# Mixer stage: value and gate projections placed between halves of the small inverse products, first batch's head products moved ahead, decay products moved from VectorE to GpSimd

## The chip, the cores and the metric

The kernel runs on one core of one Trainium2 chip. The metric is the device time of one execution in microseconds. TensorE is called PE here, VectorE DVE, ScalarE ACT, GpSimd POOL and SyncE, which issues most loads, SP.

## The reference, cut to what matters

The program is a two-layer model on two sequences (B = 2) of 128 positions and width 512, in fp32. Layer 0 has a cross-attention, a *mixer* (a gated delta rule with 16 heads of width 32) and a mixture of experts. Layer 1 has two more attentions and a feed-forward. The change is in the mixer alone. What it computes, per head:

```python
q, k, v = silu(conv(xn @ Wq)), silu(conv(xn @ Wk)), silu(conv(xn @ Wv))   # causal conv, 4 taps
q, k    = rope(l2norm(q)), rope(l2norm(k))
decay   = exp(cumulated -softplus(xn @ Wgk + dt_bias) * exp(A_log))
beta    = sigmoid(xn @ Wb + bb)
# S_t = decay_t * S_(t-1);  S_t += beta_t * k_t (v_t - S_t^T k_t)^T;  o_t = S_t^T q_t
out     = (rmsnorm(o) * gnorm_w * silu(xn @ Wg)) @ Wo
```

The kernel doesn't run the recurrence over t. For each head it forms the 128x128 matrix of key products times decay, solves a triangular system for the updates in four blocks of 32 positions (with the inverses of the 32x32 diagonal blocks computed ahead), and then multiplies by the query products times decay.

## The kernel before, in words

Each engine has its own instruction stream, written out by hand in the order in which it runs: `mixer_pe`, `mixer_act`, `mixer_dve`, `mixer_pool`. Semaphores order the engines among each other. Nothing is reordered by a scheduler, so an engine that waits holds back all that is behind it in its stream.

**Projections.** `project_mix(pe, m, cc, c)` (line 1016) is one matmul 128x128 by 128x256. m is 0 for keys, 1 for queries, 2 for values, 3 for the gate; cc is the chunk of 128 output channels (four of them), c the input chunk (four). An fp32 matmul appears in the trace as two matmul and two weight-load records, so one m is 16 matmuls and 32 records, under line 1022. The results go to PSUM banks named by `MIX_BANK`: m = 2 and m = 3 both use banks 6 and 7 before. ACT evacuates m = 1 and 2 (lines 1231, 1232), DVE runs the convolution's other taps on them (line 1303), ACT applies SiLU (line 1237). Gate chunks go through SiLU on ACT straight out of PSUM (line 1277).

**Small inverse products.** There are 128 diagonal blocks of 32x32 (`M` = 32 per group of 32 partitions). DVE inverts their 16x16 halves by columns (lines 1364, 1365), then two PE passes join the halves: `cross_rows` (line 1062) and, after a copy (line 1370), `cross_inverse` (line 1072), each 128 matmuls of 16 columns, 256 records. DVE subtracts the result (line 1374). Before, `cross_rows` stands ahead of the values' projection, and `cross_inverse` in its middle.

**Decay.** `dec` is built by PE (lines 1135, 1136) into banks 0 to 3 in turn and by ACT's Exp (line 1269). The same banks are used later.

**Head products.** `head_products(right, b)` (line 1052) multiplies krot by krot (kk) or by qrot (qk) for batch b: 16 matmuls, 32 records, into four banks (4b to 4b+3 before). DVE multiplies kk by decay (`um_dve`, line 1322), ACT copies qk out of PSUM (line 1283, four copies per batch), and DVE multiplies that by decay (`pm_dve`, line 1328, four instructions 128x1024). Before, kk of both batches and then qk of both batches stand behind the gate's projection.

**The blocked solve.** Four levels a = 0 to 3, each for both batches: `earlier` (PE, line 1167), `rest_dve` (line 1345), `within` (PE, line 1179), `solved_dve` (line 1353). Level 0 has `within` and `solved` alone. One level is 2 x 32 records of `earlier` and 2 x 32 of `within`. `pm_dve` stands in DVE's stream between `rest` and `solved` of each level, the fourth one behind the last level. The outputs (line 1200, 64 records) need pm and the last level's solution; norm, gate and the output projection (lines 1205 to 1222) follow, then the mixture of experts.

**Loads.** SP loads blocks of weights of 1 MB into a ring of four buffers (line 222); a block is requested when `blk_used` says that the one in its place has been used.

## Time and profile before

| | us |
|---|---|
| three runs | 1354.48, 1353.78, 1358.29 |
| median | 1354.48 |
| span of the profiled execution | 1357.6 |
| mixer, first instruction on PE to last of line 1222 | about 559 to 670 |
| PE busy over the span | 1313.1 (97%) |
| DVE busy | 926.7 (68%) |
| ACT busy | 718.1 (53%) |
| POOL busy | 19.2 (1%) |

The page doesn't say which of the three runs is the profiled one; its span of 1357.6 us lies 0.7 us below the longest of them. Times of trace rows are in microseconds from the span's start. In a row of a timeline the first number is the start, the second the time covered, "x" the number of records, and the bracket the idle time of the engine ahead of it with what ended it ("issue" is idle time in which no semaphore and no data was waited for). PE busy includes records that run at the lower granted clock.

### The profile page before, as it was taken

How to read it: one execution, taken by the hardware profiler on the slowest of the kernel's cores; microseconds unless marked ns; L12 is line 12 of the kernel's file. 1: busy time of each engine (PE TensorE's matmuls, PEld its weight loads, DVE VectorE, ACT ScalarE, POOL GpSimd, SP SyncE). 2: the span in 40 equal slices, each digit the busy share in tenths (PEclk: the TensorE clock that was granted, in tenths of full speed). 3: DMA queues.
4: the chain of work that ended last, by engine and by line, in shares of the span. 5: the costliest groups of instructions: out<-in, count | busy, mean ns of one | idle time of the engine just before them, and what ended most of it. 6: DMA issues, size and time to landing. Idle time of an engine off the chain costs nothing.

```text
span 1357.6 us, 23877 instructions
## 1 busy us (share of the span) xinstructions
PE 1313.1 (97%) x9930; PEld 1112.1 (82%) x9930; DVE 926.7 (68%) x1209; ACT 718.1 (53%) x887; POOL 19.2 (1%) x20
## 2 busy tenths in 40 slices
PE   9999999999999999887999999999988999999998
PEld 8899999989999996766677888888765789888886
DVE  4666665676665666675779999999777677555553
ACT  5544444554444443372357777777654444665552
POOL 0000000000000000000000000000011010000000
PEclk9999999999999999898799999999998999999999
DMA  8111011311010011201058999999960145555552
GB/s 293 38 31 36 20 36 45 124 39 36 21 36 21 21 63 63 93 34 64 33 196 332 358 351 347 346 352 344 367 259 16 63 155 187 186 185 186 185 185 78
DMA packets 50223, 197.72 MB, mean 146 GB/s; under 512 B 12112, under 2 KB 20560, under 8 KB 30416
## 3 DMA queue, kind: packets, MB, share of 16 engines
q1 hardware_dynamic: 47792, 187.41, 38.1%
q0 software_dynamic: 2336, 8.91, 1.8%
q8 instruction: 75, 1.23, 0.4%
q14 instruction: 20, 0.16, 0.0%
HBM read 195.78 MB, written 0.52 MB: 145 GB/s over the span
## 4 chain that ended last, share of the span: by engine, by line
PE 86%; DVE 8%; ACT 3%; issue 2%; DMA 1%; SPq 0%; POOL 0%; DVEq 0%; ACTq 0%
PE psum L465 13%; PE psum L435 13%; PE psum L2445 9%; PE psum L1641 8%; PE psum L492 5%; PE psum L2446 4%; PE psum L1664 4%; PE psum L517 4%; PE psum L1644 4%; PE psum L2428 3%; PE psum L1022 2%; PE psum L1667 2%; PE psum L2459 2%; PE psum L476 1%; PE psum L1678 1%
## 5 line engine op out<-in xcount | busy, mean ns | idle before, releaser
L1710 DVE TENSOR_TENSOR arena_r<-ring,arena_r 128x2048 fp32r<-128x2048 f32 x96 | 219.7, 2290 | 29.6 <-ACT arena_r L1704 29.3
L465 PE MATMUL psum<-ring_r,arena_r 128*128 128x256 f32 x1536 | 198.1, 287 | 0.7 <-DVE ring_r L300 0.7
L1704 ACT CAST arena_r<-ring 128x2048 fp32r<-128x2048 f32 x96 | 183.4, 1914 | 14.1 <-PE psum L1644 11.1
L465 PEld LDWEIGHTS psum<-ring_r,arena_r 128*128 128x128 f32 x1536 | 188.6, 191 | 1.3 <-DVE ring_r L300 1.1
L435 PE MATMUL psum<-arena_r 128*128 128x512 f32 x768 | 183.5, 394 | 0.4 <-ACT arena_r L751 0.3
L2445 PE MATMUL psum<-arena_r 128*128 128x512 f32 x512 | 181.0, 399 | 1.4 <-DVE arena_r L2510 1.4
L435 PEld LDWEIGHTS psum<-arena_r 128*128 128x128 f32 x768 | 141.6, 188 | 32.0 <-DVE arena_r L300 1.0
L2446 PE MATMUL psum<-arena_r 128*128 128x256 f32 x512 | 143.9, 281 | 0.0
L2399 DVE TENSOR_TENSOR arena_r<-ring,arena_r 128x2048 fp32r<-128x2048 f32 x43 | 98.6, 2293 | 62.1 <-ACT arena_r L2394 62.1
L1641 PE MATMUL psum<-arena_r 128*128 128x512 f32 x512 | 129.5, 395 | 1.3 <-issue 1.3
L2445 PEld LDWEIGHTS psum<-arena_r 128*128 128x128 f32 x512 | 96.3, 188 | 25.3 <-DVE arena_r L2510 1.5
L1641 PEld LDWEIGHTS psum<-arena_r 128*128 128x128 f32 x512 | 94.2, 188 | 20.4 <-issue 1.7
L772 ACT COPY arena<-psum 128x1024 f32<-128x1024 f32 x64 | 61.7, 1016 | 89.6 <-PE psum L492 89.6
L300 DVE TENSOR_TENSOR arena_r<-arena,arena_r 128x2048 fp32r<-128x2048 f32 (+4 forms) x34 | 52.1, 1538 | 79.2 <-ACT arena_r L743 52.2
L2394 ACT CAST arena_r<-ring 128x2048 fp32r<-128x2048 f32 x44 | 84.0, 1909 | 30.3 <-PE psum L2428 20.0
L2446 PEld LDWEIGHTS psum<-arena_r 128*128 128x128 f32 x512 | 96.8, 189 | 0.0
L637 DVE TENSOR_TENSOR arena<-arena,psum 128x1024 f32<-128x1024 f32 x64 | 75.2, 1216 | 24.8 <-PE psum L506 24.8
L764 ACT COPY ring<-psum 128x512 f32<-128x512 f32 x64 | 37.2, 582 | 78.7 <-PE psum L465 78.7
L779 ACT ACTIVATE arena<-arena 128x1024 f32<-128x1024 f32 x64 | 66.3, 1058 | 21.0 <-DVE arena L637 19.7
L617 DVE TENSOR_TENSOR arena<-arena 128x512 f32<-128x512 f32 (+1 forms) x128 | 71.5, 559 | 4.4
L1644 PE MATMUL psum<-arena_r 128*128 128x512 f32 x256 | 68.6, 390 | 0.0
L492 PEld LDWEIGHTS psum<-arena 64*128 64x128 f32 x1024 | 59.7, 188 | 9.9 <-issue 9.1
(337 smaller groups left out, 1900.3 us busy)
## 6 DMA issues: line engine op xcount, KB each, us to landing
ring<-in_stream SPq DMA_DIRECT2D x151, 1024.0 KB, 4.9
arena<-in_ctxT POOLq DMA_DIRECT2D x8, 1024.0 KB, 11.6
arena<-in_ctxT SPq DMA_DIRECT2D x7, 1024.0 KB, 7.9
arena<-in_wk SPq DMA_DIRECT2D x16, 256.0 KB, 3.2
wv_in<-in_wv SPq DMA_DIRECT2D x8, 512.0 KB, 3.5
arena<-in_wq SPq DMA_DIRECT2D x16, 256.0 KB, 2.7
arena<-in_wk SPq DMA_DIRECT2D x16, 128.0 KB, 3.2
arena<-in_wo SPq DMA_DIRECT2D x2, 1024.0 KB, 6.5
```

Of the source, the lines that this page charges most:

```text
L435: last = nc.tensor.matmul(bank, wk_sb[wp][:, c, w], cx[xp][kb][:, c, :], start=c == wp == xp == 0, stop=c == C - 1 and xp == 1)
L465: last = nc.tensor.matmul(bank[:, q * T:(q + 1) * T], cx[xp][kc // 4][:, c, kc % 4 * P:(kc % 4 + 1) * P], wv_sb[wp][:, c, :], start=c == w ...
L492: last = nc.tensor.matmul(psum[:, 2 * half + kc // 4, kc % 4 * P:kc % 4 * P + P], kT[j % 2][a:a + 64, k0:k0 + P], qT[a:a + 64, j % 2, half ...
L637: nc.vector.tensor_tensor(part, part, per_row(psum[:, SPREAD_BANK, 0:P], KC // 2), ALU.subtract).then_inc(shifted, 1)
L1641: nc.tensor.matmul(out, xg[xp][:, c, e, :], hi[:, c, :], start=c == xp == 0, stop=False)
L1644: last = nc.tensor.matmul(out, xg[0][:, c, e, :], lo[:, c, :], start=False, stop=c == C - 1)
L1704: nc.scalar.copy(mwhi[p % MB], ring[k % RING][:, :]).then_inc(moe_hi, 1)
L1710: nc.vector.tensor_tensor(mwlo[p % MB], ring[(BLK_MOE + p) % RING][:, :], mwhi[p % MB].bitcast(fp32), ALU.subtract).then_inc(moe_lo if p < ...
L2394: nc.scalar.copy(whi[j % 2], ring[k % RING][:, :]).then_inc(w_hi, 1)
L2399: nc.vector.tensor_tensor(wlo[j % 2], ring[(BLK_W12 + j) % RING][:, :], whi[j % 2].bitcast(fp32), ALU.subtract).then_inc(w_lo, 1)
L2445: nc.tensor.matmul(psum[:, 4 + s, :], w[0][:, c, :], src[:, :, c, :], start=c == 0, stop=False)
L2446: last = nc.tensor.matmul(psum[:, 4 + s, 0:T], w[1][:, c, :], src[:, 0, c, :], start=False, stop=c == FC - 1)
```

## The change

In words:

- PE's stream: the first chunk of the values' projection goes ahead of `cross_rows`; `cross_rows` and `cross_inverse` are cut in halves of 64 matmuls (128 records), with one chunk of a projection between the halves; turning of the queries (`turn_mix`) goes behind the whole values' projection; kk and qk of batch 0 go ahead of and behind the gate's last chunk, kk of batch 1 follows, qk of batch 1 is last.
- PSUM: the gate goes to banks 2 and 3, the inverse products to banks 0 and 1, and the batches swap places (`BASE` = (4, 0)).
- ACT's stream: the copy between the two inverse products moves from DVE to ACT; the query squares go between the evacuations; the first half of the gate's SiLU goes ahead of the values' SiLU.
- DVE's stream: the rotation of the queries goes between the halves of the values' convolution; `um_dve` of batch 0 goes ahead of the inverse's last subtraction and of `vp_dve`; `pm_dve` is gone.
- POOL's stream: `pm_pool`, the same four multiplications, behind the memsets.

```diff
-        MIX_BANK = (4, 6, 6, 6)
+        MIX_BANK = (4, 6, 6, 2)
+        ROWS_BANK, INV_BANK = 0, 1
+        BASE = (4, 0)
...
             nc.gpsimd.memset(cross_sb[:, :, HK:], 0.0).then_inc(xf_clear, 1)
+            for n in range(4):
+                pm_pool(gp, n)
...
+            if m == 2 and c == 0 and cc % 2 == 0:
+                pe.wait_ge(mix_evac, C + cc + 2)
+            if m == 3 and cc == c == 0:
+                pe.wait_ge(dec_exp, G)
...
-                    last = nc.tensor.matmul(psum[:, 4 * b + i, cc * P:(cc + 1) * P], krot[r, cc, b, :], right[r, cc, b, :],
+                    last = nc.tensor.matmul(psum[:, BASE[b] + i, cc * P:(cc + 1) * P], krot[r, cc, b, :], right[r, cc, b, :],
...
+            def project_whole(m, cc):
+                for c in range(C):
+                    project_mix(pe, m, cc, c)
+
+            halves = (range(0, M // 2), range(M // 2, M))
+            project_whole(2, 0)
             pe.wait_ge(xt_ready, 1)
-            cross_rows(4).then_inc(inv_filled, 1)
-            pe.wait_ge(mix_evac, 2 * C)
-            for cc in range(C):
-                if cc == C // 2:
-                    pe.wait_ge(xt_ready, 2)
-                    cross_inverse(5).then_inc(inv_filled, 1)
-                for c in range(C):
-                    project_mix(pe, 2, cc, c)
+            pe.wait_ge(dec_exp, 5)
+            cross_rows(ROWS_BANK, halves[0])
+            project_whole(2, 1)
+            cross_rows(ROWS_BANK, halves[1]).then_inc(inv_filled, 1)
+            project_whole(2, 2)
+            project_whole(2, 3)
+            turn_mix(pe, 1, 4)
+            pe.wait_ge(xt_ready, 2)
+            pe.wait_ge(dec_exp, 6)
+            cross_inverse(INV_BANK, halves[0])
+            project_whole(3, 0)
+            cross_inverse(INV_BANK, halves[1]).then_inc(inv_filled, 1)
+            project_whole(3, 1)
+            project_whole(3, 2)
+            pe.wait_ge(mix_evac, 3 * C)
+            pe.wait_ge(rope_ready, 2)
+            head_products(krot, 0).then_inc(kk_filled, 1)
+            project_whole(3, 3)
+            pe.wait_ge(um_ready, 1)
+            head_products(qrot, 0).then_inc(qk_filled, 1)
+            pe.wait_ge(mix_gs, 2)
             pe.wait_ge(xt_ready, 3)
-            turn_mix(pe, 1, 4)
-            pe.wait_ge(mix_evac, 3 * C)
-            for cc in range(C):
-                for c in range(C):
-                    project_mix(pe, 3, cc, c)
-            pe.wait_ge(dec_exp, G)
-            head_products(krot, 0).then_inc(kk_filled, 1)
-            pe.wait_ge(mix_gs, 2)
-            pe.wait_ge(rope_ready, 2)
             head_products(krot, 1).then_inc(kk_filled, 1)
-            for b in range(B):
-                pe.wait_ge(um_ready, b + 1)
-                head_products(qrot, b).then_inc(qk_filled, 1)
+            pe.wait_ge(um_ready, 2)
+            head_products(qrot, 1).then_inc(qk_filled, 1)
...
             silu_mix_act(act, 1)
+            act.wait_ge(inv_filled, 1)
+            act.wait_ge(xf_clear, 3)
+            nc.scalar.copy(cross_sb[:, :, 0:HK], psum[:, ROWS_BANK, :].rearrange("p (n j) -> p n j", j=HK)).then_inc(xt_ready, 1)
+            evac_mix_act(act, 2, 0)
+            evac_mix_act(act, 2, 1)
             square_mix_act(act, 1, 1)
-            for cc in range(C):
-                evac_mix_act(act, 2, cc)
+            evac_mix_act(act, 2, 2)
+            evac_mix_act(act, 2, 3)
+
+            def gate_act(i):
+                wait_mix_chunk(act, 3, 2 * i + 1)
+                nc.scalar.activation(gsT[:, 2 * i:2 * i + 2, :, :], psum[:, MIX_BANK[3] + i, :].rearrange("p (c b t) -> p c b t", c=2, b=B),
+                                     ACT.Silu).then_inc(mix_gs, 1)
+
+            gate_act(0)
             silu_mix_act(act, 2)
...
+            gate_act(1)
...
-        def pm_dve(dve, n):
+        def pm_pool(gp, n):
 
             heads = slice(n * H // 2, (n + 1) * H // 2)
-            dve.wait_ge(qk_copied, 4 * (n // 2) + 4)
-            nc.vector.tensor_tensor(pm[:, heads, :], qk[:, heads, :], dec[:, heads, :], ALU.mult).then_inc(pm_ready, 1)
+            gp.wait_ge(qk_copied, 4 * (n // 2) + 4)
+            nc.gpsimd.tensor_tensor(pm[:, heads, :], qk[:, heads, :], dec[:, heads, :], ALU.mult).then_inc(pm_ready, 1)
...
             conv_mix_dve(dve, 1, 1)
-            cross_copy_dve(dve)
             rope_start_dve(dve, 1, qrot)
+            conv_mix_dve(dve, 2, 0)
+            rope_dve(dve, 1, qrot, 4)
+            conv_mix_dve(dve, 2, 1)
+            um_dve(dve, 0)
             cross_inverse_dve(dve)
-            conv_mix_dve(dve, 2, 0)
-            conv_mix_dve(dve, 2, 1)
-            rope_dve(dve, 1, qrot, 4)
             vp_dve(dve)
-            um_dve(dve, 0)
             um_dve(dve, 1)
             for a in range(NT):
                 for b in range(B):
                     if a:
                         rest_dve(dve, a, b)
-                if a:
-                    pm_dve(dve, a - 1)
                 for b in range(B):
                     solved_dve(dve, a, b)
-            pm_dve(dve, 3)
```

Every other `4 * b` in a PSUM bank's number of the mixer becomes `BASE[b]`.

## Rows read from the trace of the kernel before

**Rows 1.** The page: span, and queue of instruction loads (packets, MB, share)

```profile
span 1357.6 us, 23877 instructions
...
q8 instruction: 75, 1.23, 0.4%
```

**Rows 2.** Timeline of PE, 598 to 640 us: start, time covered, instructions, idle before

```profile
600.33 2.22 PE L1062 MATMUL psum<-arena 16*32 16x16 f32 x139 [0.81 <-DVE arena L1420]
603.93 1.91 PE L1062 MATMUL psum<-arena 16*32 16x16 f32 x117 [1.38 <-issue]
605.76 6.28 PE L1022 MATMUL psum<-xnT,ring 128*128 128x256 f32 x16
611.97 2.29 PE L1072 MATMUL psum<-arena 32*32 32x16 f32 x251
616.57 0.24 PE L1072 MATMUL psum<-arena 32*32 32x16 f32 x5 [2.31 <-issue]
616.75 5.41 PE L1022 MATMUL psum<-xnT,ring 128*128 128x256 f32 x16
621.99 1.88 PE L1031 MATMUL psum<-arena,cst 128*128 128x512 f32 x4
623.71 7.09 PE L1022 MATMUL psum<-xnT,ring 128*128 128x256 f32 x32
630.73 2.07 PE L1052 MATMUL psum<-arena 32*128 32x128 f32 x64
...
635.51 1.17 PE L1052 MATMUL psum<-arena 32*128 32x128 f32 x32 [0.49 <-DVE arena L1322]
```

**Rows 3.** Windows: us, PE, PEld, DVE, ACT, POOL busy, granted clock, DMA share, GB/s

```profile
601.00:601.50 0.50, 0.50 (x50) 0.50 (x44) 0.50 (x3) 0.45 (x1) 0.00 (x0) 1.00 0.14 33
...
643.60:644.10 0.50, 0.50 (x32) 0.47 (x32) 0.50 (x1) 0.00 (x0) 0.00 (x0) 0.50 0.17 33
647.40:647.90 0.50, 0.50 (x42) 0.42 (x36) 0.33 (x2) 0.00 (x0) 0.00 (x0) 0.50 0.17 33
...
574.00:600.00 26.00, 23.53 (x402) 16.38 (x401) 19.90 (x47) 23.37 (x55) 0.00 (x0) 1.00 0.19 70
...
604.20:610.80 6.60, 6.60 (x124) 5.58 (x117) 2.62 (x5) 2.11 (x2) 0.00 (x0) 0.50 0.02 5
```

**Rows 4.** Timeline of DVE and ACT, 598 to 662 us

```profile
629.73 1.22 DVE L1341 TENSOR_TENSOR arena<-arena,nkp 128x1024 f32<-128x1024 f32 x1
632.04 3.42 DVE L1322 TENSOR_TENSOR arena<-psum,arena 96x1536 f32<-96x1536 f32 x2 [1.09 <-PE psum L1052]
...
635.09 4.01 ACT L1283 COPY arena<-psum 128x512 f32<-128x512 f32 x8 [3.65 <-PE psum L1052]
...
645.08 1.22 DVE L1328 TENSOR_TENSOR arena<-arena 128x1024 f32<-128x1024 f32 x1
646.33 1.29 DVE L1353 TENSOR_TENSOR arena<-psum,beta 32x512 f32<-32x512 f32 x2
```

**Rows 5.** Timeline of PE, 639 to 662 us

```profile
643.55 1.25 PE L1167 MATMUL psum<-arena 64*32 64x32 f32 x64 [1.17 <-DVE arena L1353]
...
647.08 1.26 PE L1167 MATMUL psum<-arena 96*32 96x32 f32 x64 [1.17 <-DVE arena L1353]
...
650.70 3.73 PE L1200 MATMUL psum<-arena 128*32 128x128 f32 x64 [1.27 <-DVE arena L1353]
```

**Rows 6.** Timeline of POOL and DVE around the only other SBUF-to-SBUF products on POOL

```profile
674.88 2.71 POOL L2624 TENSOR_TENSOR arena_r<-xn,arena_r 128x1024 fp32r<-128x1024 f32 x1 [115.26 <-ACT arena_r L1718]
...
1086.69 0.61 DVE L2339 SCALAR_TENSOR_TENSOR arena<-arena,lkvs 128x128 f32<-128x128 f32 x2
1087.15 4.53 POOL L2638 TENSOR_TENSOR arena_r<-ring,arena_r 128x2048 fp32r<-128x2048 f32 x1 [56.40 <-ACT arena_r L2394]
...
1087.89 4.20 DVE L2339 SCALAR_TENSOR_TENSOR arena<-arena,lkvs 128x128 f32<-128x128 f32 x2
```

**Rows 7.** Windows of the mixture of experts, columns as in rows 3

```profile
740.00:780.00 40.00, 40.00 (x185) 32.47 (x184) 35.53 (x24) 31.06 (x25) 0.00 (x0) 1.00 0.94 352
```

More of the change, by code:

```diff
@@ L1051, in head_products, with cross_rows @@
                     r = tile_rows(i)
-                    last = nc.tensor.matmul(psum[:, 4 * b + i, cc * P:(cc + 1) * P], krot[r, cc, b, :], right[r, cc, b, :],
+                    last = nc.tensor.matmul(psum[:, BASE[b] + i, cc * P:(cc + 1) * P], krot[r, cc, b, :], right[r, cc, b, :],
                                             start=True, stop=True)
             return last
-        def cross_rows(bank):
-            for n in range(M):
+        def cross_rows(bank, tiles):
+            for n in tiles:
                 for i in range(4):
@@ L1064, in cross_rows, with cross_inverse @@
             return last
-        def cross_inverse(bank):
-            for n in range(M):
+        def cross_inverse(bank, tiles):
+            for n in tiles:
                 for i in range(4):
@@ L1166, in earlier @@
                         h = 4 * cc + i
-                        last = nc.tensor.matmul(psum[tile_rows(i), 4 * b, cc * DK:(cc + 1) * DK], um[0:DK * a, b * H + h, tile_rows(a)],
+                        last = nc.tensor.matmul(psum[tile_rows(i), BASE[b], cc * DK:(cc + 1) * DK], um[0:DK * a, b * H + h, tile_rows(a)],
                                                 xw[0:DK * a, b, h * DK:(h + 1) * DK], start=True, stop=True)
@@ L1178, in within @@
                         r = tile_rows(i)
-                        last = nc.tensor.matmul(psum[tile_rows(a), 4 * b + i, cc * DK:(cc + 1) * DK], xt[r, :, (cc * B + b) * NT + a],
+                        last = nc.tensor.matmul(psum[tile_rows(a), BASE[b] + i, cc * DK:(cc + 1) * DK], xt[r, :, (cc * B + b) * NT + a],
                                                 rhs[r, b, cc, :] if a else vp[r, cc, b, 0, :], start=True, stop=True)
@@ L1199, in mixer_pe @@
                         h = 4 * cc + i
-                        last = nc.tensor.matmul(psum[tile_rows(i), 4 * b, cc * P:(cc + 1) * P], xw[:, b, h * DK:(h + 1) * DK],
+                        last = nc.tensor.matmul(psum[tile_rows(i), BASE[b], cc * P:(cc + 1) * P], xw[:, b, h * DK:(h + 1) * DK],
                                                 pm[:, b * H + h, :], start=True, stop=True)
@@ L1208, in mixer_pe @@
                 for cc in range(C):
-                    last = nc.tensor.matmul(psum[0:H, 4 * b + 1, 0:P], C_("sums")[:, cc * H:(cc + 1) * H], osq[:, b, cc, :],
+                    last = nc.tensor.matmul(psum[0:H, BASE[b] + 1, 0:P], C_("sums")[:, cc * H:(cc + 1) * H], osq[:, b, cc, :],
                                             start=False, stop=cc == C - 1)
@@ L1214, in mixer_pe @@
                 for cc in range(C):
-                    last = nc.tensor.matmul(psum[:, 4 * b + 1, cc * P:(cc + 1) * P], C_(f"heads{cc}")[0:H, :], rs[0:H, b * P:(b + 1) * P],
+                    last = nc.tensor.matmul(psum[:, BASE[b] + 1, cc * P:(cc + 1) * P], C_(f"heads{cc}")[0:H, :], rs[0:H, b * P:(b + 1) * P],
                                             start=True, stop=True)
@@ L1270, in mixer_act @@
             silu_mix_act(act, 1)
-            square_mix_act(act, 1, 1)
-            for cc in range(C):
-                evac_mix_act(act, 2, cc)
+            act.wait_ge(inv_filled, 1)
[3 more added lines that the diff above has]
+            evac_mix_act(act, 2, 1)
+            square_mix_act(act, 1, 1)
+            evac_mix_act(act, 2, 2)
[5 more added lines that the diff above has]
+            gate_act(0)
             silu_mix_act(act, 2)
-            for i in range(2):
-                wait_mix_chunk(act, 3, 2 * i + 1)
-                nc.scalar.activation(gsT[:, 2 * i:2 * i + 2, :, :], psum[:, 6 + i, :].rearrange("p (c b t) -> p c b t", c=2, b=B),
-                                     ACT.Silu).then_inc(mix_gs, 1)
+            gate_act(1)
             for b in range(B):
@@ L1444, in mixer_dve @@
                     dve.wait_ge(mix_gs, 2)
[L1445 removed]
+                nc.vector.scalar_tensor_tensor(t1[:, :, b, :], bank4(BASE[b]), gcol[:, 0:1], gsT[:, :, b, :], ALU.mult, ALU.mult)
             for b in range(B):
```

23 lines of the change are left out of this document (9 added, 14 removed).

## The prediction

> **What bounds the kernel now.** The page comes first: 97% of the span is PE busy, but the change touches only the mixer, some 110 us of 1357.6 [rows 1], so the page's shares decide nothing. I then read the windows and the timeline of PE in the mixer. In the mixture of experts behind it PE is busy 40.00 of 40 us [rows 7], and its weights are loaded as buffers come free; it does not catch up on a late mixer, and a mixer that ends earlier should move it whole. So the question is when the outputs' products (line 1200) end, at 654.43 us [rows 5].
>
> From 599.52 us (the last decay matmul's end, 600.33 less 0.81 of idle [rows 2]) to there, PE's order is a single path with these losses [rows 2]:
> - 0.81 us waiting for DVE's last transpose, ahead of the first inverse products;
> - 1.38 us idle within them and 2.31 us within the second ones, both put down to "issue": no semaphore, no data. The first stops after 140 records, the second after 251;
> - the granted clock is 0.50 (1.2 GHz) from 604.2 to 610.8 us [rows 3], right behind the first idle stretch, and, by the durations, for a part of the time behind the second. Eight matmuls (16 records) of the values' projection take 6.28 us there and 5.41 us the second time, against 7.09 us for sixteen of the gate's at full clock [rows 2]: 0.785 and 0.68 against 0.443 us each.
>
> What is an "issue" stop? The page shows 75 packets of 1.23 MB in an instruction queue, 16.4 KB each [rows 1]. One lies in 601.0 to 601.5 (33 GB/s over half a microsecond, nothing else moving), and PE goes on at 603.93 [rows 2, 3]. Between the two stops are 117 + 16 + 251 = 384 records of each kind [rows 2], and three further packets: one packet is about 128 pairs of matmul and weight load. So I read it thus: PE holds two pages of 128 pairs; when it enters one, the next is ordered, and that one is there some 3.7 us after the entry (packet about 1 us after the entry, ready 2.7 us after the packet). In the solve's levels packets lie in 643.6 to 644.1 and 647.4 to 647.9, again 3.5 to 3.9 us apart [rows 3]. A page with 128 inverse products is eaten in 2.0 us (16 ns a pair, 2.22/139) or 1.1 us (2.29/251) [rows 2], and then PE stands.
>
> **The projections between the halves.** A half is 128 pairs; a projection chunk is 8 pairs and 4 x 0.443 = 1.77 us at full clock. The new path, marks in us of this trace:
> - 599.52 to 601.3: first values' chunk. It fills the 0.81 wait.
> - first half of the rows: 2.05, to 603.35. The page ends 3 pairs into the next chunk and the following is ready at about 603.9 (entered as before). Chunk to 605.1, second half's first 123 pairs to 607.1, next page at 607.6, half ends at 607.7.
> - two chunks 3.55 and the turning 1.72 (1.88 less the overlap of the first): 613.0. First half of the inverse, 1.15, to 614.1; gate's chunk to 615.9; 94 pairs of the second half to 616.7; the page entered at about 613.6 gives 617.3; done at 617.6.
> - two gate chunks to 621.1, kk of batch 0 1.15 to 622.3, last gate chunk to 624.1.
> So all four projections' chunks and one kk are behind PE at 624.1, where the kernel before ends the gate at 630.8 [rows 2]. What is left of stops is 0.5 + 0.6 us, against 3.7. The saving needs the clock to stay high, which I come to below.
>
> **Head products.** The first multiplication on DVE (half of 3.42, 1.7 us [rows 4]) runs beside the last gate chunk: 622.4 to 624.1. Then qk of batch 0 624.2 to 625.4, its ACT copies (half of 4.01) to 627.4; kk of batch 1 to 626.5. On DVE the inverse's subtraction (0.7, half the elements of a 1.22), a transpose and a scaling of 128x1024 (1.22 each, 1.25 taken for the first) [rows 4] stand ahead of the second multiplication: 627.4 to 629.1. Before, that DVE work lay hidden under the gate's projection; now its second part is on the path. qk of batch 1 then ends at 630.35 (before: 635.51 + 1.17 = 636.68 [rows 2]), its copies at 632.45 (639.1). The lead is 6.6 us: the head products' reorder itself saves 1.15 us of PE and one multiplication's wait, and pays part of it back to DVE's order.
>
> **Moved for nothing.** The copy on ACT costs 0.6 there, as a 128x512 read of PSUM by ACT does, and DVE isn't needed; ACT's evacuations behind it are late by that and DVE's convolution has about 4 us left before kk of batch 0 is there. Banks: 0 and 1 are free after the fifth and sixth Exp, long done; 2 and 3 after the eighth, done at 600.2. The loads requested when a projection is done come 6 to 10 us sooner and collide with nothing.
>
> **Decay products on POOL.** DVE does them in 1.22 each [rows 4]; POOL took 2.71 for the same shape [rows 6]. The first two start at 627.4 and end at 632.8, the others end by 638.3, and the outputs want them at 642 or later: hidden, with 4 us to spare. On DVE each of the three inside the levels is on the path. Level to level is 647.08 - 643.55 = 3.53 us [rows 5]. Without the product I make it 2.65: half each of earlier's 1.25, within's (about as long: as many records) and solved's 1.29 make 1.87 [rows 4, 5], a rest of 0.3 (a quarter-size piece, by the 1.22), and four hand-overs of 0.12 (estimates). That would give 3 x 0.88 = 2.6 us. But a level is 128 pairs, one page. Its packets are already 3.5 to 3.9 us apart, and the page for level 3, ready near 646.5, was only 0.5 us ahead of its use at 647.08. At 2.65 us a level PE eats faster than pages come. By my count page ends lie 5 pairs into levels 1, 2 and 3 and into the outputs; pages come at 629.0, 636.7, 640.4 and 644.1. Level 0 is solved at 633.9, level 1 at 636.55; level 2 waits for 636.7, ends at 639.8; level 3 waits for 640.4 and ends at 643.5; the outputs wait for 644.1 and, 59 of 64 pairs at 58 ns, end at 647.55. So I take 0.3 us for the move out of DVE, between 0 (the page period) and 2.6 (none).
>
> **The sum.** 654.43 - 647.55 = 6.9 us. Profile: span 1357.6 - 6.9 = 1350.7. The median of the runs shown lies 3.1 under the span, so 1354.48 - 6.9 = 1347.6 us.
>
> **Two rules of the Trainium skill.** The page of before has DVE's line 2339 at 4.20 us for two instructions beside a product on POOL that runs 1087.15 to 1091.68, and 0.61 us without it [rows 6]. By the Trainium skill, SBUF — State Buffer, Who interferes with whom, a DVE instruction with two SBUF inputs and a POOL instruction that reads SBUF exclude each other for the whole instruction. By that rule, the trace agrees, line 1341 is the one at risk here; it would start 1.3 us ahead of POOL's first product, so POOL would wait and nothing be lost, while the solve's DVE steps each read PSUM and have one SBUF input.
> The Trainium skill, Runtime: NRT & Kernel Launch, Instruction fetch mechanics, says PE holds 128 KiB of instructions and that crossing a 16 KiB boundary is mostly hidden. The stops [rows 2] speak against it; if it held in the new order, the result would be rival A's.
>
> **Rivals.**
> A. *Pages don't bind the new order* (the ordering starts earlier in a page than I think, or two may be under way). Then the stops of 0.5 + 0.6 go and the levels run at 2.65: the outputs end near 645 - 0.6 = 644.4, gain 10: 1344.5. For it: my count of page ends may be off by some pairs, and PE idles before level 0, so pages can be full. Against: the even distances of the packets.
> B. *The clock falls again.* The fall at 604.2 follows a stretch with products of 16 columns and idle time, and these products are still there. If the chunk behind the first half and the two behind it run at 0.785, 12 x 0.342 = 4.1 us go, or 2 to 4 when only some do: gain 3 to 5, 1350.5. Against: 574 to 600 us has small products, an idle 2 us and granted clock 1.00 throughout [rows 3].
> C. *The changed order does nothing*: solve and DVE's order take back what PE gains, since um of batch 1 now stands behind vp and inverse. If silu or the rotation is late too by 4 us, kk of batch 0 waits, gain 0 to 3: 1353. Against: rows show those DVE pieces short.
> D. *Slower.* The interleaving turns a burst of low activity into a lasting one, and the granted clock stays 0.50 through all 32 matmuls of values and gate: 32 x 0.342 = 10.9 us, less the 6.9: 4.0 us slower, 1358.5. It decides from 6.9/0.342 = 20 matmuls at the low clock on. Against: the projections alone, dense, raised the clock after 610.8 [rows 3].
>
> **Chances.** My forecast (gain 5.5 to 8.5) 0.42, A 0.18, B 0.24, C 0.11, D 0.05. Three runs of before spread over 0.33%, so 0.3%, 4.1 us, is what can be told from no change. Faster by more: forecast, A and about 0.16 of B: 0.76. Within: the rest of B and C: 0.19. Slower: 0.05. The range leaves out A's far end and D: 1343.0 to 1353.0; my forecast's own is 1346 to 1349.
>
> **What would show it.** Timeline of PE: values' first chunk at 599.5 without a wait; no issue stop over 1 us in the inverse products; gate done near 624; qk of batch 1 ended near 630.4. Windows: granted clock 1.00 from 600 to 628 (B: 0.50 somewhere in 604 to 611). In the levels, issue stops ahead of line 1167 or inside it, packets 3.7 apart and 3.5 to 3.7 us a level (A: 2.65). POOL: four products near 2.7 each; if any ends behind level 3, the decay products are on the path. It is wrong if the mixture of experts starts 7 us earlier and the total doesn't fall by as much.

## The result and the profile after

The changed kernel took 1350.37 us, median of nine runs (1346.89 to 1353.59), against 1355.87 for the kernel before, median of nine beside it (1351.94 to 1358.69): 5.5 us less, ratio 0.996 with a 95% interval of 0.9945 to 0.9975. Timed a second time it gave 1350.49 against 1356.15, ratio 0.9965 (0.9949 to 0.998). The forecast was 6.9 us less. In time it was 1347.6 us, with 1346 to 1349 as its own range: the measured 1350.37 is inside the range for the total (1343.0 to 1353.0) and above the forecast's own. Of the 2.8 us between them 1.4 is the baseline, three runs of the kernel before having a median of 1354.48 and nine one of 1355.87. One of the twelve executions of the changed kernel's second timing took 3289.45 us and is in no ratio; the median without it is 1350.22.

The profiled execution of the changed kernel has a span of 1347.7 us, 9.9 us under the one of before [rows 1]. Of these 7.2 us lie in the mixer between the start of its first matmuls (559.36 before, 560.03 now) and the end of the outputs' products. Only 5.0 of the 7.2 lie behind the last decay matmul, where the forecast's sum begins (+54.91 against +49.94 in the table below); PE's order ahead of it is the same in both kernels. The rest lies elsewhere; a second pair of profiles, below, shows that a good part of it is not the change's.

PE's timeline of the mixer in the changed kernel's first profile, in the place of [rows 2, 5] (start, time covered, instructions, idle before):

```profile
597.85 1.89 PE L1030 MATMUL psum<-xnT,ring 128*128 128x256 f32 x8
599.67 2.01 PE L1070 MATMUL psum<-arena 16*32 16x16 f32 x128
601.61 1.99 PE L1030 MATMUL psum<-xnT,ring 128*128 128x256 f32 x8
603.54 2.02 PE L1070 MATMUL psum<-arena 16*32 16x16 f32 x128
...
610.85 1.27 PE L1080 MATMUL psum<-arena 32*32 32x16 f32 x128
...
613.98 0.97 PE L1080 MATMUL psum<-arena 32*32 32x16 f32 x93
616.13 0.49 PE L1080 MATMUL psum<-arena 32*32 32x16 f32 x35 [1.18 <-issue]
616.55 5.41 PE L1030 MATMUL psum<-xnT,ring 128*128 128x256 f32 x16
...
629.74 1.24 PE L1060 MATMUL psum<-arena 32*128 32x128 f32 x32 [2.73 <-DVE arena L1350]
...
636.51 0.32 PE L1186 MATMUL psum<-arena 64*32 64x32 f32 x4 [0.16 <-DVE arena L1381]
637.03 1.07 PE L1186 MATMUL psum<-arena 64*32 64x32 f32 x60 [0.20 <-issue]
...
639.54 0.32 PE L1186 MATMUL psum<-arena 96*32 96x32 f32 x4 [0.35 <-DVE arena L1381]
640.77 1.07 PE L1186 MATMUL psum<-arena 96*32 96x32 f32 x60 [0.90 <-issue]
...
643.39 0.64 PE L1219 MATMUL psum<-arena 128*32 128x128 f32 x4 [0.45 <-DVE arena L1381]
644.33 3.41 PE L1219 MATMUL psum<-arena 128*32 128x128 f32 x58 [0.30 <-issue]
```

An "issue stop" is idle time of PE inside a run of its instructions that no semaphore and no data explains. The first inverse products run without one, their wait and the 1.38 us are gone; in the second the stop is 1.18 us instead of 2.31. In the levels there are now issue stops that [rows 5] do not have, each after exactly four records of `earlier`, and again after four of the outputs. Windows of the changed kernel (columns as in rows 3) show where the clock was low, right behind the stop in the second inverse, and a 16 KB packet (33 GB/s over half a microsecond) ahead of the last two stops:

```profile
617.00:620.40 3.40, 3.40 (x10) 2.74 (x9) 0.00 (x0) 0.50 (x2) 0.00 (x0) 0.51 0.02 5
...
638.00:638.50 0.50, 0.50 (x36) 0.45 (x34) 0.29 (x1) 0.00 (x0) 0.00 (x0) 0.50 0.17 33
641.60:642.10 0.50, 0.50 (x35) 0.41 (x29) 0.36 (x2) 0.00 (x0) 0.00 (x0) 0.50 0.15 33
```

DVE and POOL, in the place of [rows 4, 6]: the second multiplication starts behind the inverse's subtraction, transpose and scaling; two decay products take 4.65 us on POOL, 2.33 each, and the other two as long from 633.15.

```profile
623.13 1.75 DVE L1350 TENSOR_TENSOR arena<-psum,arena 96x1536 f32<-96x1536 f32 x1 [7.31 <-PE psum L1060]
624.81 0.67 DVE L1397 TENSOR_TENSOR arena<-arena,psum 128x512 f32<-128x512 f32 x1
625.40 1.23 DVE L1368 STREAM_TRANSPOSE arena<-arena 128x1024 f32<-128x1024 f32 x1
626.67 1.23 DVE L1369 TENSOR_TENSOR arena<-arena,nkp 128x1024 f32<-128x1024 f32 x1
627.93 1.75 DVE L1350 TENSOR_TENSOR arena<-psum,arena 96x1536 f32<-96x1536 f32 x1
...
628.31 4.65 POOL L1356 TENSOR_TENSOR arena<-arena 128x1024 f32<-128x1024 f32 x2 [68.02 <-ACT arena L1311]
```

### The profile page after: what moved, and what is told of

It is laid out like the page before. It is cut to its first block, busy times and chain, and to the rows that moved or that the text cites. A ratio compares the mean times of both kernels' runs of the same rounds, so it can differ in the third digit from the quotient of the medians.

```text
span 1347.7 us, 23879 instructions
## 1 busy us (share of the span) xinstructions
PE 1307.0 (97%) x9930; PEld 1107.0 (82%) x9930; DVE 921.4 (68%) x1204; ACT 718.7 (53%) x888; POOL 28.5 (2%) x24
## 3 DMA queue, kind: packets, MB, share of 16 engines
q8 instruction: 75, 1.23, 0.4%
## 4 chain that ended last, share of the span: by engine, by line
PE 87%; DVE 7%; ACT 2%; issue 2%; DMA 2%; SPq 0%; POOL 0%; DVEq 0%; ACTq 0%
PE psum L465 13%; PE psum L435 13%; PE psum L2464 9%; PE psum L1660 8%; PE psum L492 5%; PE psum L2465 5%; PE psum L1683 4%; PE psum L517 4%; PE psum L1663 4%; PE psum L2447 3%; PE psum L1030 2%; PE psum L1686 2%; PE psum L2478 2%; PE psum L476 1%; PE psum L1697 1%
## 5 line engine op out<-in xcount | busy, mean ns | idle before, releaser
L1729 DVE TENSOR_TENSOR arena_r<-ring,arena_r 128x2048 fp32r<-128x2048 f32 x96 | 219.7, 2290 | 29.6 <-ACT arena_r L1723 29.4
```

Source lines behind the costliest of these rows:

```text
L1729: nc.vector.tensor_tensor(mwlo[p % MB], ring[(BLK_MOE + p) % RING][:, :], mwhi[p % MB].bitcast(fp32), ALU.subtract).then_inc(moe_lo if p < ...
```

## The experiments

Ten kernels were run, the two known ones among them; nine were timed in several rounds, each beside runs of the kernel before on its chip, and its ratio is to those. Medians taken beside different runs of the kernel before are compared by ratio, since that kernel's own medians went from 1353.13 to 1356.15 between them. Marks of one profile each are taken from PE's timeline: D is the end of the last decay matmul; then, after D, the end of the gate's projection (G), of batch 1's qk (Q) and of the outputs' products (O). "Start to O" begins at the mixer's first matmuls. The table is made of starts plus durations.

| kernel | G | Q | O | start to O | median, us | ratio to before (95%) |
|---|---|---|---|---|---|---|
| before, 1st profile | 31.28 | 37.16 | 54.91 | 95.07 | 1355.87 | |
| before, 2nd profile | 29.10 | 34.99 | 52.69 | 92.86 | 1355.75 | 1.0002 (0.9983-1.0021) |
| changed, 1st profile | 26.97 | 32.97 | 49.94 | 87.92 | 1350.37 | 0.996 (0.9945-0.9975) |
| changed, 2nd profile | 25.00 | 31.58 | 47.84 | 87.57 | 1350.49 | 0.9965 (0.9949-0.998) |
| e1 products back on DVE | 26.96 | 32.88 | 50.36 | 88.75 | 1353.27 | 0.9991 (0.9974-1.0007) |
| e2 inverses in one piece | 29.66 | 35.58 | 52.65 | 93.04 | 1356.76 | 1.0017 (0.9998-1.0036) |
| e3 head products late | 23.70 | 29.58 | 46.82 | 85.20 | 1348.99 | 0.9956 (0.9937-0.9975) |
| e4 before, products on POOL | 27.58 | 33.46 | 50.26 | 90.03 | 1353.68 | 0.9991 (0.9975-1.0007) |
| e5 page ends shifted | 27.49 | 33.48 | 49.65 | 91.37 | 1354.1 (one run) | |
| e6 quarters | 24.37 | 31.21 | 48.81 | 86.97 | 1349.24 | 0.9966 (0.995-0.9983) |
| e8 late heads and quarters | 23.26 | 29.08 | 46.49 | 84.34 | 1345.93 | 0.9935 (0.9915-0.9955) |
| e9 e8 and tile products spread | 23.26 | 29.08 | 45.60 | 85.75 | 1345.69 | 0.9944 (0.9924-0.9965) |

Two things can be read from the table before any single run. From D, the changed kernel's O is 54.91 - 49.94 = 4.97 us sooner in the first pair of profiles and 52.69 - 47.84 = 4.85 in the second: the two pairs agree there, although each kernel's own two profiles differ by 2.1 to 2.2. And Q to O, the solve with its copies and products, takes 17.5 to 17.75 us in the three profiles with the decay products on DVE and 16.2 to 17.6 in the nine with them on POOL.

### e1: the decay products back on DVE

```diff
-            for n in range(4):
-                pm_pool(gp, n)
...
                         rest_dve(dve, a, b)
+                if a:
+                    pm_dve(dve, a - 1)
                 for b in range(B):
                     solved_dve(dve, a, b)
+            pm_dve(dve, 3)
```

> The changed kernel with the decay products back on DVE, between rest and solved of each level as before; all else as changed. Changed kernel's marks, from the end of the last decay matmul on PE (598.01 us): gate's projection done +26.97, qk of batch 1 done +32.97, outputs' products (line 1219) done +49.94. Page theory (PE gets a page of 128 pairs every 3.7 us): levels take 3.7 with or without the products on DVE, so the outputs' end moves by 0 to 0.7 us (the fourth product behind the last level is 1.2 on DVE's side but is waited for only by batch 1), and the idle time of PE put down to issue in the levels shrinks from 1.4 us to under 0.6. Rival (the products on DVE are on the path): outputs' end 2.6 to 3.5 us later. Total: 0 to 1 us over the changed kernel, or 2.6 to 3.5.

PE's timeline of this kernel, levels 2 and 3:

```profile
638.44 1.25 PE L1184 MATMUL psum<-arena 64*32 64x32 f32 x64 [1.17 <-DVE arena L1379]
...
641.96 1.26 PE L1184 MATMUL psum<-arena 96*32 96x32 f32 x64 [1.17 <-DVE arena L1379]
```

The levels are back to 641.96 - 638.44 = 3.52 us with no issue stop; O comes 0.42 us later than in the changed kernel's like-clocked profile. In the changed kernel they took 3.03 us (636.51 to 639.54) and 3.85 (to 643.39, the outputs' start). Most of what DVE gave up in the levels, the pages took: in the trace the page theory holds and the rival's 2.6 us are not there. The total doesn't say so. The median is 2.8 us above the changed kernel's (3.5 to 4.2 by the ratios, whose intervals hardly overlap), where 0 to 1 was expected by the theory and 2.6 to 3.5 by the rival. The profiled executions differ by as much: spans of 1350.5 us here and 1347.7 and 1347.2 for the changed kernel. Of that, 0.8 to 1.2 us lie between start and O, and 1.4 to 2.2 behind O, where no line differs between the two kernels (701.2 us from O to the end against 699.8 and 699.0).

### e2: both inverse products in one piece

```diff
-            cross_rows(ROWS_BANK, halves[0])
-            project_whole(2, 1)
-            cross_rows(ROWS_BANK, halves[1]).then_inc(inv_filled, 1)
+            cross_rows(ROWS_BANK, range(M)).then_inc(inv_filled, 1)
+            project_whole(2, 1)
...
-            cross_inverse(INV_BANK, halves[0])
-            project_whole(3, 0)
-            cross_inverse(INV_BANK, halves[1]).then_inc(inv_filled, 1)
+            cross_inverse(INV_BANK, range(M)).then_inc(inv_filled, 1)
+            project_whole(3, 0)
```

> The changed kernel with both small inverse products in one piece again (256 records each), the projection chunk behind each instead of between its halves. Page theory: after about 131 records of the first a stop of 1.5 to 2 us, then one of about 1 near its end or in the chunk behind it; about 2.3 us in the second (1.18 in the changed kernel). Sum 3 to 4 us later at the gate's end, and the clock granted after 604 falls to 0.50 for a window at least, 1 to 3 us more. Outputs' end and total 3 to 6 us later. Rival (the gain comes from the order and the banks, not from the spreading): under 1.5 us.

```profile
602.00 3.84 PE L1070 MATMUL psum<-arena 16*32 16x16 f32 x256
605.78 7.23 PE L1030 MATMUL psum<-xnT,ring 128*128 128x256 f32 x24
...
614.65 2.12 PE L1080 MATMUL psum<-arena 32*32 32x16 f32 x230
619.69 0.60 PE L1080 MATMUL psum<-arena 32*32 32x16 f32 x26 [2.92 <-issue]
620.22 6.76 PE L1030 MATMUL psum<-xnT,ring 128*128 128x256 f32 x24
```

The second inverse stops for 2.92 us and both projections of 24 records behind the products take 7.23 and 6.76 us where e3's 24 at full clock take 5.45: the clock fell behind each. The first inverse did not stop, against the expectation. The second's stop is at the place in the stream where the changed kernel has its own: there 128 + 8 + 93 = 229 pairs behind the start of the products, here 230, with the projection chunk moved out from between. O comes 2.7 us later and the median lies 6.3 us higher, at the kernel before's; the ratios' intervals are apart. The spreading carries the change's gain: with everything else of the change and without it nothing is won. How its price divides into stops and low clock, one profile can't say.

### e3: the head products in the old order

```diff
-            head_products(krot, 0).then_inc(kk_filled, 1)
             project_whole(3, 3)
-            pe.wait_ge(um_ready, 1)
-            head_products(qrot, 0).then_inc(qk_filled, 1)
+            head_products(krot, 0).then_inc(kk_filled, 1)
             pe.wait_ge(mix_gs, 2)
             pe.wait_ge(xt_ready, 3)
             head_products(krot, 1).then_inc(kk_filled, 1)
+            pe.wait_ge(um_ready, 1)
+            head_products(qrot, 0).then_inc(qk_filled, 1)
             pe.wait_ge(um_ready, 2)
...
-            um_dve(dve, 0)
             cross_inverse_dve(dve)
             vp_dve(dve)
+            um_dve(dve, 0)
             um_dve(dve, 1)
```

> The changed kernel with the head products behind the whole gate's projection in the old order (kk 0, kk 1, qk 0, qk 1) and DVE in its old order (inverse, values' transpose and scaling, then both multiplications). The gate ends 1.15 us sooner, at +25.8. Then kk 0 and kk 1 to +28.1; DVE is free, its multiplications at +27.1 to +28.9 and +30.6, qk 0 at +30.0, qk 1 at +31.8 to 32.0. If so qk 1 is done 1 us SOONER than in the changed kernel and only the first batch's copies are later (qk 0 copied at +32.1, qk 1 at +34.1 as against +35.1). So the expectation from the traces: outputs' end within 1 us, either side. Rival (the early head products are worth something of their own, as the change means): 1 to 3 us later.

DVE's timeline of this kernel, and then PE's:

```profile
618.42 0.69 DVE L1397 TENSOR_TENSOR arena<-arena,psum 128x512 f32<-128x512 f32 x1 [0.55 <-PE psum L1080]
621.90 1.25 DVE L1368 STREAM_TRANSPOSE arena<-arena 128x1024 f32<-128x1024 f32 x1 [2.80 <-ACT arena L1256]
623.18 1.23 DVE L1369 TENSOR_TENSOR arena<-arena,nkp 128x1024 f32<-128x1024 f32 x1
624.99 3.42 DVE L1350 TENSOR_TENSOR arena<-psum,arena 96x1536 f32<-96x1536 f32 x2 [0.58 <-PE psum L1060]
```

```profile
618.30 5.45 PE L1030 MATMUL psum<-xnT,ring 128*128 128x256 f32 x24
623.68 2.07 PE L1060 MATMUL psum<-arena 32*128 32x128 f32 x64
626.80 1.17 PE L1060 MATMUL psum<-arena 32*128 32x128 f32 x32 [1.05 <-DVE arena L1350]
628.46 1.17 PE L1060 MATMUL psum<-arena 32*128 32x128 f32 x32 [0.49 <-DVE arena L1350]
```

The same three pieces are done by 624.41, under the gate's projection and the first head products, and the two multiplications follow each other. Q is at +29.58 against +31.58 in the changed kernel's second profile, which kept its clock through the gate as this one did (0.65 of the 2.0 us is that profile's qk of batch 1 at the lower clock, 1.82 instead of 1.17). The other 1.3 us: the gate ends 1.3 sooner without a head product in front of its last chunk, against that the four head products behind it take 1.2 more than the three there, and PE waits for DVE 1.05 + 0.49 us instead of 2.73. So in the traces the early head products cost 1.3 us at full clock instead of bringing something. The median is 1.4 to 1.5 lower, 0.5 to 1.2 by the ratios, with intervals that overlap: the totals alone don't show it. That the old order is no worse was expected; its lead in the trace is larger than expected.

### e4: the kernel before with the decay products on POOL

Its edit is the part `pm_pool` of the change, alone.

> The kernel before with the decay products moved to POOL alone. Page theory: the levels go from 3.53 us to 3.5 to 3.7 us each, with issue stops of 0.2 to 1 us appearing in front of or inside line 1167's products; outputs' end 0 to 1 us sooner (what remains is the last product's 0.2 and page slack at the start). Rival (DVE is the bound and pages come in time): 2.6 to 3 us sooner. Total the same way.

```profile
599.58 3.86 PE L1064 MATMUL psum<-arena 16*32 16x16 f32 x256
...
641.67 0.32 PE L1169 MATMUL psum<-arena 96*32 96x32 f32 x5 [0.33 <-DVE arena L1355]
642.45 1.06 PE L1169 MATMUL psum<-arena 96*32 96x32 f32 x59 [0.46 <-issue]
```

Q to O is 16.8 us against 17.75 and 17.7 in the two profiles of before: 0.9, not 2.6 to 3. The median is 0.8 us under that of the kernel before beside it, which the interval doesn't tell from nothing. The stops that were foretold appear, inside line 1169's products and, 0.59 us, inside the outputs. The rest of its lead in the trace lies ahead of Q, and one part of it teaches something: the first inverse products run through, where both profiles of before stop after 139 records. The windows of this kernel (columns as in rows 3) say why:

```profile
598.60:599.10 0.50, 0.50 (x3) 0.19 (x1) 0.50 (x2) 0.50 (x1) 0.00 (x0) 1.00 0.12 33
601.00:601.50 0.50, 0.50 (x48) 0.50 (x45) 0.50 (x2) 0.50 (x1) 0.00 (x0) 1.00 0.00 0
```

Its packet came in 598.6 to 599.1, ahead of the products' start at 599.58; in the first profile of before it came in 601.0 to 601.5, behind their start at 600.33 [rows 2, 3]. In both profiles of before PE stood in the wait for DVE (0.81 and 0.73 us) and the packet came only behind it; here DVE was done before PE, and the packet came while the decay matmuls still ran. DVE's last transpose ended at 600.27 in the first profile of before and at 597.75 here, and the packet came 0.9 and 1.1 us behind it. I read that as PE's stream being read on through a wait as soon as it is met, whatever PE is still at work on. With a page ready 2.2 to 2.9 us after its packet, this one was there when its 140th product was due, 2.2 us behind 599.58. PE's and DVE's code up to there is the same in both kernels, so the missing stop is not this edit's doing but its timing's.

### Second profiles of both kernels

> The kernel before, unchanged, for a second profile of it. Its first profile ran the mixer from the first gates' matmul (559.36) to the experts' first products (line 1570, 683.20) in 123.84 us; the one with only the decay products moved took 117.5, the changed kernel 116.0. If the first profile was an unlucky one (PE at 1.2 GHz in other places, stops between pages in other places), this one takes 117.5 to 121 and the difference of the medians (5.5 us) is the true effect; if it was typical it takes 123 to 125 again and the medians understate. In either case the issue stop in the second inverse products (2.3 us) is there again.

> The changed kernel, unchanged, beside the others on one chip. Total 4 to 7 us under the kernel before. In the trace the same issue stops at the same records: 93 into the second half of the second inverse, 4 into line 1186 of levels 2 and 3, 4 into line 1219. The granted clock's low stretches may lie elsewhere; if they fall outside the gate's projection, gate done at +25.1 instead of +26.97.

The kernel before took 680.48 - 560.17 = 120.3 us from the mixer's first matmuls to the experts' first products (line 1570), 3.5 less than in its first profile. Its second inverse stopped for 2.00 us. The first profile of before lay high within its own spread. The changed kernel's second profile:

```profile
616.33 0.97 PE L1080 MATMUL psum<-arena 32*32 32x16 f32 x93
618.21 0.49 PE L1080 MATMUL psum<-arena 32*32 32x16 f32 x35 [0.91 <-issue]
618.63 3.72 PE L1030 MATMUL psum<-xnT,ring 128*128 128x256 f32 x16
```

The stops stand at the same records, 93 here and 4 in level 3 and the outputs, with other lengths; the one expected in level 2 is absent. This time the two gate chunks take 3.72 us at full clock instead of 5.41. By "start to O" the two profiles of before average 93.97 us and the two of the changed kernel 87.75: 6.2 us, beside 5.5 of the medians and 6.9 of the forecast. The 2.7 us by which the first spans differ outside this stretch sit at about 1035 to 1042, in the next layer; the windows of the second profile of before, and then the same place of the changed kernel's:

```profile
1035.00:1041.80 6.80, 6.43 (x10) 2.75 (x10) 4.00 (x10) 4.45 (x25) 0.00 (x0) 0.50 0.01 2
```

```profile
1025.00:1045.00 20.00, 16.08 (x107) 8.97 (x105) 15.66 (x37) 14.11 (x70) 0.00 (x0) 1.00 0.01 3
```

The granted clock is low there in both profiles of before and, from 1041.5 to 1044.9 (0.51), in e1's: the three with the decay products on DVE, and in none of the other nine. But two of the nine have a low stretch of their own a little earlier, where neither before nor the changed kernel has one: e4 at 998.6 to 1005.4 (0.51) and e2 at 1001.7 to 1005.1 (0.51). So low stretches move about in that layer with the products on POOL too, which speaks for timing and not for the products themselves; it is not shown. They can hold a part of what e1 loses behind O.

### e5: page ends moved by 64 records

```diff
             cross_inverse(INV_BANK, halves[0])
+            cross_inverse(INV_BANK, range(M // 4, M // 2))
             project_whole(3, 0)
```

> The changed kernel with a quarter of the second inverse products issued twice (32 matmuls, 64 records more, same results), 0.57 us of PE work, ahead of the gate's first chunk. Page theory: every later page end comes 64 pairs earlier in the stream. The stops that were 4 records into earlier (line 1187) of levels 2 and 3 are now 4 to 5 records into within (line 1199) of levels 1, 2 and 3, and the stop 93 records into the second half of the inverse is now about 29 into it. Rival (the stops belong to those instructions: weight shapes of 64 and 96 rows, bank turns): they stay 4 records into earlier. Outputs' end within 1.5 us of the changed kernel's.

```profile
618.68 0.43 PE L1080 MATMUL psum<-arena 32*32 32x16 f32 x29
620.29 1.02 PE L1080 MATMUL psum<-arena 32*32 32x16 f32 x99 [1.18 <-issue]
...
643.17 1.13 PE L1199 MATMUL psum<-arena 32*32 32x32 f32 x60 [0.42 <-issue]
...
646.63 1.13 PE L1199 MATMUL psum<-arena 32*32 32x32 f32 x60 [0.49 <-issue]
```

The stop that stood after 93 records of the second half now stands after 29, exactly 64 sooner; those of levels 2 and 3 have left `earlier` and stand inside `within`, with 60 of 64 records still to go. The stops belong to places in the instruction stream, not to instructions. That was the theory's sharpest test. Level 1 shows no stop, though one was expected. The instruction queue has 76 packets here and 75 in the profiles of the changed kernel.

### e6: quarters instead of halves

```diff
-            cross_inverse(INV_BANK, halves[0])
-            project_whole(3, 0)
-            cross_inverse(INV_BANK, halves[1]).then_inc(inv_filled, 1)
-            project_whole(3, 1)
-            project_whole(3, 2)
+            for n in range(3):
+                cross_inverse(INV_BANK, range(n * M // 4, (n + 1) * M // 4))
+                project_whole(3, n)
+            cross_inverse(INV_BANK, range(3 * M // 4, M)).then_inc(inv_filled, 1)
```

> The changed kernel with one edit: the second inverse products in quarters of 64 records with a gate chunk between each; the head products stay in the changed order. No issue stop in the second inverse (0.9 to 1.2 us in the changed kernel), no low granted clock in the gate's projection. From the last decay matmul: gate done +25.0 (changed kernel +26.97 and +25.0 in its two profiles), outputs' end 0.9 to 2.5 us sooner than the changed kernel's mean of the two. Total 1 to 2 us under the changed kernel (1350.5), so 1348.5 to 1349.5. If the late head products were the whole gain of the best version, it stays at 1350 to 1351.

```profile
618.88 0.74 PE L1080 MATMUL psum<-arena 32*32 32x16 f32 x64
...
627.39 2.09 PE L1060 MATMUL psum<-arena 32*128 32x128 f32 x32 [2.73 <-DVE arena L1349]
```

No stop and no low clock up to the gate's end, +24.37. But O comes only 0.6 and 0.95 us sooner by "start to O" (86.97 against 87.57 and 87.92), by the mark from D no sooner than the mean of the two (48.81 against 48.89), where 0.9 to 2.5 was expected, and the median is 1.2 lower: behind DVE's 2.73 us the clock fell, qk of batch 1 took 2.09 us instead of 1.17, and level 3's stop was 1.18. In ratio to before the two kernels are the same; a gain of its own is not shown.

### e8: late head products and quarters together

The edits of e3 and e6, and in DVE's stream:

```diff
-            cross_inverse_dve(dve)
             vp_dve(dve)
+            cross_inverse_dve(dve)
             um_dve(dve, 0)
             um_dve(dve, 1)
```

> A better version, if the readings hold: the changed kernel with the head products in the old order behind the whole gate (as in the experiment that came out 1.4 us under the changed kernel), the second inverse products in quarters of 64 records with a gate chunk between each, and the values' transpose and scaling ahead of the inverse's subtraction on DVE. 64 records of 8.7 ns and a chunk of 1.8 us are 2.3 us for 72 pairs, 4 us for a page: no stop there at all (0.9 to 1.2 before), and no idle stretch for the clock to fall behind. From the last decay matmul: gate done +24.9, qk of batch 1 done +29.3, outputs' end +45.8 (changed kernel +49.9; late heads alone +46.8). Total 0.5 to 2 us under late heads alone, 2 to 4 under the changed kernel. Rival (quarters don't matter since the late-heads run happened to keep its clock): equal to late heads alone within 0.5.

```profile
624.72 1.17 PE L1060 MATMUL psum<-arena 32*128 32x128 f32 x32 [0.98 <-DVE arena L1349]
626.39 1.17 PE L1060 MATMUL psum<-arena 32*128 32x128 f32 x32 [0.49 <-DVE arena L1349]
```

The median is 1345.93 us, 4.6 under the changed kernel and 10.2 under the kernel before, both beside it (ratio to before 0.9935, 0.9915 to 0.9955). Its slowest run (1347.63) is below the changed kernel's fastest (1348.47): it beats both, by more than the 2 to 4 us expected against the changed kernel. There is no stop in the second inverse, G is at +23.26, sooner than expected, Q at +29.08; O at +46.49, 0.7 later than expected: the levels' stops stay (0.43, 0.90 and 0.59). Beside e6, which has the early head products, Q is 31.21 - 29.08 = 2.1 us sooner, 0.9 of it e6's low clock: the second pair of kernels in which the old order is ahead (e8 also has the values' transpose and scaling moved on DVE).

### e9: the tile products spread too

```diff
             place(beta[:, :], 2).then_inc(placed, 1)
+            for c in range(C // 2, C):
+                project_mix(pe, 1, 1, c)
+            for c in range(C):
+                project_mix(pe, 1, 2, c)
             tile_products(4, range(G // 2, G)).then_inc(kkd_filled, 1)
```

> The best version so far (late head products, quarters) with 12 records of the queries' projection moved ahead between the two halves of the key tile products (line 1051), where every profile has an issue stop of 1.7 to 2.4 us after 250 records. Page theory: the stop is time until the next page is there, so work put in front of it replaces it: the stop shrinks by the 2.7 us of the chunks, to zero, PE reaches the decay matmuls about 1.7 us sooner or waits there for DVE (its inverse starts 0.6 to 0.9 us later). Time from the first gates' matmul to the last decay matmul 37.0 to 38.5 us as against 38.0 to 40 in the others; total 0 to 1.7 us under the best version. Rival (the stop is a fixed cost of those products): the stop stays at 1.7 to 2.4 and the total rises by up to 1.

```profile
583.37 2.86 PE L1030 MATMUL psum<-xnT,ring 128*128 128x256 f32 x12
586.15 1.29 PE L1051 MATMUL psum<-arena 32*32 32x32 f32 x128
...
591.13 1.10 PE L1144 MATMUL psum<-arena,cst 128*128 128x512 f32 x2 [1.39 <-issue]
```

The stop of 1.7 to 2.4 us in those products is gone, as the page theory said; in its place PE is idle for 1.39 us ahead of the decay matmuls. The profile calls that issue, but PE also waits there by semaphore for DVE's copy of the placed sums (line 1361), which ends at 591.02, 0.11 us ahead of PE's start, so it is probably a wait for DVE, as was expected for one of the two outcomes. From the first matmuls to D it took 40.2 us, where 37.0 to 38.5 was expected and e8 took 37.9; a part of that is the granted clock of 0.53 in 560 to 567, against 1.00 in e8, ahead of the edit. Median 1345.69: no gain over e8 that can be told.

## Why the prediction came out as it did

- **What bounds the mixer and what an issue stop is.** Right. Pages of 128 pairs, one ordered when the one before is entered: e5 moved the stops by the 64 pairs added, e2 made the second inverse's stop 2.92 us, e6 and e8 removed it, e9 removed another.
- **The projections between the halves.** The mechanism was right and carries the gain (e2). Sizes: the first inverse was to stop for 0.5 us and didn't. The page seems to be ordered when PE's stream is *read* up to it, ahead of the work (e4's packet); with the wait for DVE gone it is read sooner. The second was to stop for 0.6 and stopped for 1.18 and 0.91.
- **The clock.** I took full clock throughout for the sum and had the fall as rival B, behind the first inverse. It fell behind the second, from 617.0 to 620.4: two chunks took 5.41 us in the changed kernel's first profile and 3.72 at full clock in its second. That is most of the distance of its G (+26.97) from the forecast's 624.1 - 599.52 = 24.6. Rival B had the mechanism and the wrong place, and its number: it said 1350.5 for a gain of 3 to 5. The time measured is that, and not the forecast's. Whether the clock made it so isn't shown: one of the two profiles has the fall in the gate, the other doesn't.
- **Head products.** The step that failed. I wrote that the reorder "itself saves 1.15 us of PE and one multiplication's wait, and pays part of it back to DVE's order". The 1.15 us were never there to save: PE has the same head products to do, and one put ahead of the gate's last chunk ends the gate by as much later (+25.00 against +23.70 in e3). Nor was a wait saved: PE waited 2.73 us for DVE where the old order has 1.05 + 0.49, since DVE's three pieces (0.67, 1.23, 1.23) stand between the two multiplications. Together Q is 1.3 us later at full clock (e3). The forecast's marks held that price, Q at 630.35 - 599.52 = +30.8 against the measured +31.58, of which 0.65 is low clock; what I didn't do is to compare them with the old order behind the same projections, which is +29.6.
- **Decay products on POOL.** Hidden, as said, at 2.33 us each instead of 2.71. The levels became bound by pages as said: Q to O was to be 647.55 - 630.35 = 17.2 and was 16.97, stops of four records into levels 2, 3 and the outputs where five were counted. Moved alone it brings 0.9 us in the trace (e4), undone it costs 0.4 to 1.2 up to O (e1); I had 0.3. By the medians it is 0.8 and 2.8, and what it is worth in all stays open. The scaling that was named as at risk beside POOL (line 1341 before, 1369 now) ended at 627.90 and POOL's first product began at 628.31: they missed each other by 0.4 us, where 1.3 was expected, and nothing was lost.
- **The sum.** 6.9 was forecast, 6.2 is the mean of the profiles' stretch and 5.5 the medians'. Counted from D, as the forecast was, both pairs give 4.9. It missed by 2 us in either of two ways. In the first pair O came at +49.94 instead of 647.55 - 599.52 = +48.03, mostly by the low clock. In the second it came at +47.84, but the kernel before also did better, +52.69: its first profile, from which the sum starts, had a second low stretch (5.41 us for 16 records, 3.72 in the second profile) and longer stops. That +47.84 is so near +48.03 is in part luck: Q was 0.75 later than forecast and the levels with the outputs 0.9 faster. A is refuted by the levels' stops, C by the medians (its gain was 0 to 3; measured are 5.5, interval 3.4 to 7.5). D had it the wrong way round: the low clock follows both inverses in e2, where nothing stands between the halves, and there the gain is gone.

What stays open: why e1 loses 1.4 to 2.2 us behind O, in code that it shares with the changed kernel, and whether the low clock at 1035 to 1045 follows from where the decay products are.

## What to carry to other kernels

An idle time put down to issue, inside a run of hundreds of very short PE instructions, can be a matter of instruction supply (look for a 16 KB packet 2 to 3 us ahead of its end; e9's idle 1.39 us has none there and is probably a semaphore's): put long instructions between stretches of short ones until a page of them lasts as long as a page takes to come (in e6 and e8, 72 pairs in 2.6 us ran without a stop). Before a serial chain is shortened on one engine, count the instructions that it feeds to another: two levels of 128 pairs took 7.15 us with the products on DVE and still 6.1 to 7.2 without them, held by their pages. And when work is moved ahead on one engine, ask what on the other then stands between two links of the chain; e3 undid such a move and was faster in its trace, and not slower in its median.

## What the runs showed of the hardware

- A page of 16.4 KB, 128 pairs of matmul and weight load: from level 1 to the outputs its packets are 3.4 to 4.2 us apart in the nine profiles with the products on POOL, and PE goes on 2.2 to 2.9 us after the packet at each of the mixer's stops within short products (601.2 to 603.93 in before, 615.96 to 618.21 in the changed kernel's second profile). The length of a stop differs between profiles of one kernel (1.18 and 0.91; 0.20 and none in level 2), its place doesn't.
- The same kernel has its low-clock stretches in different places: the gate's chunks took 5.41 us in one profile of the changed kernel and 3.72 in the other. One profile against one profile said 9.9 us where the medians say 5.5.
- A product of two 128x1024 fp32 operands takes 2.33 us on POOL and none of DVE's steps beside it, each with a PSUM operand, was longer for it (line 1381 for one: 0.68, as before at 637.92 and 639.91).
